# Four of eight decision trees take their leaf by a row fetched per token instead of by a dense product

## The reference, cut to what matters

```python
h = patchify(x) @ W.T + b                                # 196 tokens of 256 an image
h = h + attn(_layernorm(h))                              # norm, u/v/base, rotary q and k, relu^2 scores, o
def ffn(x):                                              # x = _layernorm(h)
    logits = x @ W_in.T + b_in                           # 8 trees x 255 nodes
    decisions = (logits > 0); acts = silu(logits)
    current = 0
    for d in range(7):                                   # walk down: left or right by the decision
        current = (current - (2**d - 1)) * 2 + decisions[current] + 2**(d + 1) - 1
        dmap = dmap + one_hot(current, 255)
    return (acts * dmap) @ W_out.T
h = h + ffn(_layernorm(h))
```

## Time and profile before

| | us |
|---|---|
| median of 3 runs | 2263.17 |
| lowest and highest | 2258.26, 2264.08 |
| the profiled execution | 2262.11 |
| its span (first to last instruction) | 2260.3 |
| mean granted clock of PE, as a share of full speed | 0.991 |

### The profile page before, as it was taken

How to read it: one execution, slowest core, us unless ns; L and a number is a source line. 1 busy time by engine, 2 the same in 40 slices (tenths; PEclk the granted TensorE clock), 3 DMA queues, 4 the chain that set the end, 5 groups by cost and what they waited for, 6 DMA issues and landing times.

```text
span 2260.3 us, 37987 instructions
## 1 busy us (share of the span) xinstructions
PE 2204.4 (98%) x13248; PEld 2078.2 (92%) x13248; DVE 1721.6 (76%) x3534; ACT 1091.2 (48%) x1992; POOL 292.8 (13%) x361
## 2 busy tenths in 40 slices
PE   6799999999999999999999999999999999999999
PEld 5799999999999999999999999999999999999998
DVE  5677787778787777877777877787777778777876
ACT  4344554444554445544445544445444455444453
POOL 4631111001111001110011110011100111100110
PEclk8899999999999999999999999999999999999999
DMA  3110000000000000000000000000000000000000
GB/s 115 53 45 9 21 28 28 28 28 0 28 28 28 28 14 14 28 28 28 28 0 28 28 28 28 18 11 28 28 28 28 0 28 28 28 28 21 7 18 15
DMA packets 38403, 58.89 MB, mean 26 GB/s; under 512 B 4879, under 2 KB 32497, under 8 KB 38385
## 3 DMA queue, kind: packets, MB, share of 16 engines
q1 hardware_dynamic: 38384, 58.66, 8.8%
HBM read 45.80 MB, written 12.85 MB: 26 GB/s over the span
## 4 chain that ended last, share of the span: by engine, by line
PE 86%; DVE 8%; issue 3%; ACT 2%; POOL 1%; DMA 0%; DVEq 0%; SPq 0%; ACTq 0%; POOLq 0%
PE front L904 11%; PE front L906 11%; PE front L905 11%; PE out_acc L904 8%; PE hid_ps L904 8%; PE hid_ps L905 8%; PE hid_ps L906 8%; PE out_acc L905 8%; PE out_acc L906 8%; PE front L939 3%; PE front L932 3%; DVE tok_major L689 2%; PE hid_ps L1080 2%; DVE tok_major L257 2%; DVE v_lo L593 1%
## 5 line engine op out<-in xcount | busy, mean ns | idle before, releaser
L904 PE MATMUL hid_ps<-ffn_x,in_lo 128*128 128x392 f32 x1024 | 368.4, 360 | 5.3 <-POOL in_lo L338 4.1
L904 PE MATMUL out_acc<-hid_hi,outw_lo 128*128 128x392 f32 x1024 | 367.4, 359 | 0.0
L905 PE MATMUL hid_ps<-ffn_x,in_hi 128*128 128x392 f32 x1024 | 350.9, 343 | 0.0
L906 PE MATMUL hid_ps<-ffn_x,in_hi 128*128 128x392 f32 x1024 | 350.2, 342 | 0.0
L905 PE MATMUL out_acc<-hid_lo,outw_hi 128*128 128x392 f32 x1024 | 348.8, 341 | 0.0
L906 PE MATMUL out_acc<-hid_hi,outw_hi 128*128 128x392 f32 x1024 | 348.5, 340 | 0.0
L498 ACT ACTIVATE hid<-hid_ps,leaf_col 128x392 f32<-128x392 f32 x256 | 149.3, 583 | 357.1 <-PE hid_ps L906 315.6
L344 POOL TENSOR_TENSOR inv_root<-to_root,minus_half 98x8 f32<-98x8 f32 x64 | 106.3, 1661 | 1609.6 <-DVE to_root L633 918.6
L773 DVE SCALAR_TENSOR_TENSOR hid<-hid_ps,hid 128x392 f32<-128x392 f32 x512 | 261.7, 558 | 40.9 <-PE hid_ps L1080 40.9
L382 ACT ACTIVATE hid_hi<-hid 128x784 fp32r<-128x784 f32 x256 | 219.6, 858 | 151.1 <-PE out_acc L906 113.5
L593 DVE TENSOR_TENSOR hid_lo<-hid,hid_hi 128x784 fp32r<-128x784 f32 x256 | 248.3, 970 | 17.2 <-ACT hid_hi L382 17.2
(11 more groups left out here) (111 smaller groups left out, 4924.3 us busy)
## 6 DMA issues: line engine op xcount, KB each, us to landing
x_raw<-x SPq DMA_DIRECT2D x192, 196.0 KB, 2.4
out<-out_stage SPq DMA_DIRECT2D x32, 392.0 KB, 2.4
late_raw<-in_w SPq DMA_DIRECT2D x8, 256.0 KB, 2.8
late_raw<-out_w SPq DMA_DIRECT2D x8, 128.0 KB
tok_major<-tok_w SPq DMA_DIRECT2D x3, 256.0 KB, 4.7
u<-uv_w SPq DMA_DIRECT2D x1, 576.0 KB, 4.4
late_raw<-o_w SPq DMA_DIRECT2D x2, 256.0 KB, 5.3
late_raw<-out_w SPq DMA_DIRECT2D x8, 64.0 KB
```

The costliest lines, as they stand in the source:

```text
L904: pe.matmul(out, w[1], x_parts[0], start=start, stop=False)
L905: pe.matmul(out, w[0], x_parts[1], start=False, stop=False)
L906: return pe.matmul(out, w[0], x_parts[0], start=False, stop=stop)
```

## The change

Trees 0 to 3 (`GATHERED = 4`) lose their dense leaf half. Their in_w and out_w keep only the inner nodes (`halves(t)` is 1 for them, 2 for trees 4 to 7), so `tree_logits` is six matmuls instead of twelve and each `tree_out` three instead of six. In their place, for each of these trees s and each unit:

- DVE makes `taken` (decision and visited) beside the mask; PE multiplies it by the node's step weights (`find_leaf`, four matmuls with one column) to get each token's leaf number in PSUM; ACT writes it as an integer (`leaf_number`).
- POOL issues four indirect DMAs (`fetch_rows`, one for each token group): each token's partition gets its leaf's row of `table` in HBM, 513 numbers: input weights, bias, output weights. `leaf_rows` has eight slots, that is, two trees.
- DVE takes the dot product of the row with the token's normed vector (`leaf_dots`), ACT takes silu (`leaf_silu`), DVE adds activation times output row into `leaf_sum` (`leaf_add`). Once a unit PE turns the sum back (`turn_leaf_sum`, eight transposes) and DVE adds it to the kept h (`leaf_keep`).

Besides, `norm_apply` moves from DVE to ACT, with a small product `shift` on POOL ahead of it; ACT takes silu of base three times (two of them straight into the swapped halves) and also does `scale_base`, so `swap_base` goes. The second norm writes a buffer of its own, `normed2`. The late ring has two buffers, the table is built in the first body, and late pieces are split between the fetches of the second. The order of each engine's body is written anew.

```diff
-LATE, LATE_RING = 512, 4
+LATE, LATE_RING = 512, 2
+GATHERED = 4
+ROW_IN, ROW = D + 1, 2 * D + 1
+ROW_SLOTS = 2 * GATHERED
+def halves(t):
+    return 1 if t < GATHERED else 2
...
             def norm_roots(n, which):
...
+                pool.wait_ge(roots_ok, 2 * n + which + 1)
+                pool.tensor_tensor(shift[:, :], moments[:, 4], inv_root[:, 0:GROUPS], ALU.mult).then_inc(shift_ok, 1)
...
+            def fetch_rows(i, s):
...
+                pool.wait_ge(leaf_at_ok, GATHERED * i + s + 1)
+                if GROUPS * (s + 1) > ROW_SLOTS or not first(i):
+                    pool.wait_ge(leaf_added, GROUPS * (GATHERED * i + s + 1) - ROW_SLOTS)
...
+                pool.tensor_tensor(held[:, :], minus_half[:, 0:1], minus_half[:, 0:1], ALU.mult).then_inc(held_ok, 1)
+                for g in range(GROUPS):
+                    pool.indirect_dma_start(
+                        row_slot(s, g), None, table,
+                        bass.IndirectOffsetOnAxis(ap=leaf_at[:, s, g:g + 1], axis=0),
+                        element_offset=s * P * ROW).then_inc(row_landed(i, s, g)[0], 16)
...
+            def norm_apply(n, which, g):
...
+                act.activation(dst, turned(g // 2)[:, g % 2], ACT.Identity, bias=shift[:, g:g + 1],
+                               scale=inv_root[:, g:g + 1]).then_inc(normed_ok, 1)
...
+            def leaf_number(i, s):
...
+                act.wait_ge(leaf_found, GATHERED * i + s + 1)
...
+                act.activation(leaf_at[:, s], hid_ps[0:HALF, s % 2, 1, T:T + GROUPS],
+                               ACT.Copy).then_inc(leaf_at_ok, 1)
...
+                if t < GATHERED:
...
+                    dve.scalar_tensor_tensor(taken[:, :], hid_ps[:, t % 2, 1, 0:T], VISITED[0],
+                                             decide[:, t % 2], ALU.is_ge, ALU.mult).then_inc(taken_ok, 1)
...
+            def leaf_dots(i, s):
...
+                for g in range(GROUPS):
+                    dve.wait_ge(*row_landed(i, s, g))
+                    w = row_slot(s, g)[:, 0:ROW_IN]
+                    dve.tensor_tensor_reduce(w, w, normed2[:, g], 1.0, 0.0, ALU.mult, ALU.add,
+                                             leaf_logit[:, s, g:g + 1]).then_inc(dotted, 1)
+
+            def leaf_add(i, s):
...
+                dve.wait_ge(leaf_active, GATHERED * i + s + 1)
...
+                    if s == 0:
+                        dve.tensor_scalar(leaf_sum[:, g], w, act, None, ALU.mult).then_inc(leaf_added, 1)
+                    else:
+                        dve.scalar_tensor_tensor(leaf_sum[:, g], w, act, leaf_sum[:, g],
+                                                 ALU.mult, ALU.add).then_inc(leaf_added, 1)
...
+            def find_leaf(i, s):
...
+                pe.wait_ge(taken_ok, GATHERED * i + s + 1)
+                pe.wait_ge(masked, HALVES * i + halves_before(s + 1))
...
+                for g in range(GROUPS):
+                    last = pe.matmul(hid_ps[0:HALF, s % 2, 1, T + g:T + g + 1], taken[:, g * HALF:(g + 1) * HALF],
+                                     leaf_steps[:, :], start=True, stop=True)
+                last.then_inc(leaf_found, 1)
```

More of the change, by code:

```diff
@@ L836, in body @@
                 residual(n, 0)
-                mask(i, 3)
                 residual(n, 1)
-                hid_low(i, 2)
-                if first(n):
-                    build_toward()
-                swap_base(n)
-                scale_base(n, 1)
-                scale_base(n, 0)
+                decisions(i, 4)
+                hid_low(i, 3)
+                decisions(i, 5)
+                leaf_dots(i, 1)
                 rotate_q(n)
@@ new lines, in turn_leaf_sum @@
+            def turn_leaf_sum(i):
+                if i is None:
+                    return
+                pe.wait_ge(leaf_added, GROUPS * GATHERED * (i + 1))
+                pe.wait_ge(masked, HALVES * i + halves_before(TREES - 1))
+                for m in range(DC):
+                    for g in range(GROUPS):
+                        last = pe.transpose(hid_ps[:, 0, m, g * HALF:(g + 1) * HALF],
+                                            leaf_sum[:, g, m * P:(m + 1) * P], ident[0:HALF, 0:HALF])
+                last.then_inc(leaf_turned, 1)
```

482 lines of the change are left out of this document (329 added, 153 removed).

## The result

The changed kernel takes 2259.69 us (median of 17 runs, 2257.78 to 2261.76) against 2263.33 us of the kernel before in the same runs (17, 2257.75 to 2264.6): a ratio of 0.9983, with a 95% interval of 0.9977 to 0.999. That is 0.17% faster, where 1.6% was forecast, and less than the 0.3% that I had set as the bound of no change. The time lies inside the range of the prediction.

The account below looks back on a forecast made before the run. PE, busy 98%, was taken to bound the kernel before. Span 2260.3 - 39 (thirty units) + 4 (start +3, end +1) = 2225.3, time 2227; own range 2185 to 2254, 8 in 10 for 2135 to 2335.

Parts of the forecast that it names:

- The undisturbed unit: Steady unit meeting no low clock; forecast as three stretches, 10.4 + 12.9 + 44.3 = 67.6 us, 1.3 less than before.
- third stretch: Steady unit from the base projection to the next final: forecast 44.3 us, against 44.6 before.
- mix 0: PE's wait in the stretch behind the base projection: scores come 0.6 us late and mix 0 another 0.9.
- Thirty units give -39: Steady units: 30 periods of 67.6 us in place of 68.9 take 39 us off the span.
- Tail: End of the span, 40.5 us before: +1 forecast, no front to hide the leaf chain, though 48 slots go there.
- Head: Start of the span, 152.8 us before: +3 forecast (-3 to +15), for ring, table and POOL's splits between fetches.
- the estimate beside the sum: POOL's fetches: from the skill's about 1 us to first byte, a tree's four take 4 us; sum left unchanged.
- PE stays the bound: Rival, chance 0.13: waits mostly covered, a unit takes PE's 61.9 us plus some 2; total 2119.
- DVE dearer: Rival, chance 0.15: a dot product at 0.74 us puts 3.5 us into the third stretch; unit 71.1, total 2332.
- late fetches: Rival, chance 0.13: at 2.3 us a fetch on POOL, k's rotation is 5.8 us late; unit 72, total 2360.
- the lock: Rival, chance 0.05: POOL's fetches and DVE lock each other out, 8.4 us a unit; unit 76, total some 2480.
- No change: Rival, chance 0.09: the three stretches of the steady unit lose just what PE gains; total within 0.3%.

## Why the prediction was right or wrong

**The undisturbed unit: right.** Forecast 10.4 + 12.9 + 44.3 = 67.6, measured 67.63. The forecast counts the wait of the first logits to the third stretch, and these logits start 2.5 us behind the final: cut there, the short unit has 10.5, 12.7 and 44.4. PE's busy time in it is 62.6 (61.9 forecast), DVE's 56.8 (59.1).

**The waits: right in place and size.** Find of tree 2: 2.0 forecast, 2.00 measured. First logits 1.3 against 1.40; `turn_normed` 0.8 against 0.65; mix 0: 0.9 against 0.4.

**What failed is the step from the unit to the total**, "Thirty units give -39". It prices a wait of PE at its own length. Here a wait of 2.0 us also brought the lower clock to what follows, in 14 of 30 units, at 1.45 us each: 14 x 1.45 = 20 us, 0.7 a unit. Nothing in the kernel before showed it, since its only regular wait was 0.65 us; but the low clock of its head did show that the lower level exists, and I had no rival for it. Filling one wait moves the falls to the next; with both covered they are gone and the total is 2229.8. That this is so close to the forecast 2227 is partly chance: that unit is a different one, at the same length.

**Tail: mis-sized.** +1 forecast, +8.1 measured. 1.4 to 2.7 of it go with fetches that nothing hides (run without them). The clock there is 0.89 against 0.99; how much of the rest that makes was not separated. **Head:** +3 forecast, +5.7 measured, inside its own range; the waits for the splits grew from 4.1 to 12.7 us. Together the three add up: 21 (periods) + 7 + 3 = 31 us over the forecast span of 2225.3, which gives 2256.3.

**The single prices.** The groups of the whole trace after, costliest first (busy us, mean ns; idle before):

```profile
L464 POOL DMA_INDIRECT leaf_rows<-leaf_table,leaf_at x512 | 514.4, 1005 | 167.2 <-issue 167.2
L967 DVE CUSTOM_DVE_ANT_0 leaf_rows<-leaf_rows,leaf_x 98x257 f32<-98x257 f32 x512 | 189.6, 425 | 2.2 <-DMA leaf_rows<-leaf_table,leaf_at 2.1
L984 DVE SCALAR_TENSOR_TENSOR leaf_sum<-leaf_rows,leaf_act,leaf_sum 98x256 f32<-98x256 f32 x384 | 159.9, 477 | 0.3 <-ACT leaf_act L681 0.3
...
L552 ACT ACTIVATE tok_major<-tok_major,xn_scale 98x256 f32<-98x256 f32 x128 | 54.6, 513 | 0.0
```

A fetch is busy 1.0 us and has a gap of 0.3 behind it, 1.3 from start to start (1.1 forecast; its threshold was 1.6). A dot product has a slot of 0.35 (0.45 forecast): reading the sum overlaps in full. That is the 16 x 0.1 = 1.6 us by which DVE stayed under the forecast, with 0.7 elsewhere. A tree's four fetches take 5.1, where the estimate beside the sum had 4. A find is four matmuls, 0.16 us from the first to the next product, half of what I took. The scalings on ACT take 0.70 (0.5 forecast), and still bound nothing.

**The rivals.** PE stays the bound, DVE dearer, late fetches and the lock did not come true as priced. The lock least of all: without fetches the unit has the same length. (The price of the late fetches was off by its own terms: 6.4 + 8 x 2.3 + 3.6 - 23 is 5.4 us, not 5.8. The forecast does not rest on it.) No change is what the total shows, but not by its mechanism, that the stretches lose what PE gains; they kept 1.3 us a unit, and the clock took half.

## What to carry over

When a change takes work from an engine that was always busy and turns it into waits, price each regular wait of TensorE twice: its length, and the low clock that may follow it; here 1.4 us of wait were enough, and behind 1.07 us it did not fall. Such falls have to be removed all at once, since with one wait covered they turn up behind the next, so an edit that shows no gain alone can be worth 1.3% with another. And where a kernel fetches many rows, run the unaltered kernel beside every variant, and look for signals that come later than the work that gives them.

## What was not expected of the hardware

- The low clock behind waits of 2.0 and of 1.4 us, in some units and not in others of the same shape, at a price of 1.2 to 1.6 us a fall; behind regular waits of 1.07 us and less it was not seen.
- Idle matmuls of 120 columns, 0.11 us each, whose sums nobody reads kept the clock up behind the wait that they filled; with the other regular wait shortened too they made the kernel faster.
- TensorE's signals 2.3 us late in four runs with row fetches and prompt in all others, with the same program in one of the four.
- The power over 98 x 4 values on POOL takes 1.74 us in the second norm now, against 1.02 before. VectorE's `hid_low` with two SBUF inputs runs beside it from 1179.02 to 1179.99, the power from 1179.15:

```profile
1179.15 1.75 POOL L436 TENSOR_TENSOR inv_root<-to_root,minus_half 98x4 f32<-98x4 f32 x1 [20.03 <-DVE to_root L833]
```

```profile
1179.02 0.97 DVE L793 TENSOR_TENSOR hid_lo<-hid,hid_hi 128x784 fp32r<-128x784 f32 x1
```

The Trainium skill (SBUF — State Buffer, Who interferes with whom) names this pair, a VectorE instruction with two SBUF inputs against a GpSimd one that reads SBUF; the 0.7 us agree with it, and lie in the chain that the first logits wait for. No run of the changed kernel is without them.
